# A GRU between two expert layers: chunk 0's early sums in f16 parts, idle f16 passes, and new places for y, routing and evacuation

## The chip, the cores and the metric

The kernel runs on one core of a Trainium2 chip. The metric is the device time of one execution in microseconds (us); the runs of a kernel are summed up by their median. The core's engines work side by side, each in the order of its own instruction stream, and wait for one another by semaphores: PE (TensorE, matmuls), ACT (ScalarE), DVE (VectorE), POOL (GpSimd) and SP (which issues DMAs).

## What is computed

Sixteen sequences of 128 time steps with 128 features, in two layers with a residual each:

```python
h  = gelu(x @ W.T + fc_bias + (x @ v / 128) @ u.T / 16 + cond)     # low-rank adapted, exact gelu
x  = x + relu(h @ q(W1).T + b1) @ q(W2).T + b2                      # q: weights rounded to -1, 0, 1
def step(H, xt):                                                    # a GRU over the 128 time steps
    Z  = sigmoid(xt @ Wxz.T + bxz + H @ Whz.T + bhz)
    R  = sigmoid(xt @ Wxr.T + bxr + H @ Whr.T + bhr)
    Ht = tanh(xt @ Wxh.T + bxh + R * H @ Whh.T + bhh)
    H  = Z * H + (1 - Z) * Ht
    return H, H @ Whq.T + bhq
y  = scan(step, cond, x)
e  = argmax(y @ router_w.T + router_b)                              # one of 32 experts for each token
x  = x + relu(relu(y @ w1[e] + b1[e]) @ w2[e] + b2[e])
```

## The kernel before, in words

Features lie on the 128 partitions, and a column is one (time, sequence) pair, so a time step is 16 columns. The 128 steps are cut into K = 8 chunks of 16 steps, 256 columns each. The GRU is one chain of 128 steps; all other work is hung into the chain's gaps. While chunk k runs its steps, the first layer (gelu and ternary FFN) is worked out for chunks k+1 to k+3, and routing and experts for chunk k-1. The order on every engine is written out by hand: each step of each engine calls functions that look at k and t (the step in the chunk) and issue what stands there.

A step goes like this. PE adds x's share to the sum for the early copy of the reset gate (`early_input`, L948), then the old state's products with the gates' weights (`product`, L1082, and `early_product`, L959). ACT takes three sigmoids (L454 r_early, L458 the gate r into `factors`, L460 z), DVE forms r * H in f16 (`terms`, L837) and, by a scan, the rounding error of that (`parts`, L866). PE multiplies both with Whh into the candidate's sum; ACT makes keep = 1 - z (L482) and tanh (L487); DVE forms the two halves z * H and keep * tanh of the new state, each as an f16 value and an f16 remainder (`zh_p` L871 and L876, `m_p` L880 and L883), and PE goes on with those.

The other work has three places in a step on PE: `before` (behind the gates' products, ahead of `terms`), `between` (`terms` and `parts`), and `behind` (behind `parts`, while tanh and the state's update run); in chunk 0 these are `first_before`, `first_between` and `first_behind`. On DVE the places are behind `terms` and ahead of the scan, `wide(k, t, 0)` in the middle (ahead of `zh_p`'s remainder, L876) and `wide(k, t, 1)` at the step's end; chunk 0 has `first_early` and `first_wide`. On ACT they are behind z, ahead of keep and tanh, and behind tanh.

Numbers of full precision go through PE as two f16 parts (value and remainder, `_hi` and `_lo`), with three products. In chunk 0 those parts of x do not exist, and its products with x, in `early_input` and `project_first` (L963), are f32 matmuls on x itself. `spare_passes`, `spare_hidden` and `stream` (L1130) are matmuls of 256 f16 columns into halves of PSUM banks that nobody reads; they compute nothing that is used. `x1_evacuate` (L525) takes the ternary FFN's sum out of the O bank and adds the residual; `early_input` writes to the same bank, and where the bank is being read (`out_bank_read`, L1126) PE first waits for `zh_lo`, which DVE signals behind the evacuation. `y_high` (L364) makes y's f16 value from the Whq product, `y_low` its remainder; `best_logit`, `best_places` and `first_place` find the best expert; `turn_masks` (PE) and `turned_masks` (ACT) make the mask. `expert_low` makes the remainder of an expert tile, half a tile at a time, and PE's `expert_hidden` for tile c waits for both halves of tile c - 2 (L1006).

## Time and profile before

| | |
|---|---|
| median of 3 runs | 259.83 us (259.51 to 261.93) |
| the profiled execution | 263.02 us, of which the span is 261.2 us |
| PE busy in the span | 250.5 us (96%), 3854 matmuls |
| DVE, ACT busy | 218.3 us (84%), 162.7 us (62%) |
| granted clock of PE, mean over the span | 0.928 |

All engines' times are counted from the span's start. A busy time of PE is modelled from when matmuls start, and matmuls overlap, so the distance from one matmul's start to the next one's tells more of what it costs than its own duration. The granted clock is the share of full speed (2.4 GHz) that PE was given. The step borders in the tables below are the starts of r's sigmoid (L458).

### The profile page before, as it was taken

Reading aid. Unit: us, or ns where it says so; the run is one execution under the profiler, and the core shown is the slowest. Engines: PE = TensorE matmul, PEld = TensorE weight load, DVE = VectorE, ACT = ScalarE, POOL = GpSimd, SP = SyncE. Lnnn points to the kernel's source line nnn. Section 1 sums busy time; section 2 is a strip of 40 time slices with the busy share of each in tenths; the row PEclk is TensorE's granted clock in tenths of the full one; section 3 lists DMA queues with packets and bytes.
Section 4 is the critical chain, followed back from the end, with each engine's and each line's share of the span. In section 5 each row is a group of like instructions: output and inputs, shape, how many; then the busy total and the mean of one; then the engine's idle time right before and its main releaser. Section 6 shows DMA issues by size and latency. Waiting matters only on the chain.

```text
span 261.2 us, 10662 instructions
## 1 busy us (share of the span) xinstructions
PE 250.5 (96%) x3854; PEld 204.6 (78%) x3854; DVE 218.3 (84%) x1528; ACT 162.7 (62%) x826; POOL 15.2 (6%) x29
## 2 busy tenths in 40 slices
PE   6999899999999999999999999999999999999996
PEld 6978788788877788788877777777877777777775
DVE  5776566789998989988998999898988988788983
ACT  3455455557665866677666766587657766556652
POOL 4872000000000000000000000000000000000000
PEclk9995555559999999999999999999999999999999
DMA  7900000000000000000000000000000000000000
GB/s 245 360 15 6 0 3 1 3 0 4 4 3 4 23 1 3 4 24 3 4 4 20 4 3 4 4 23 4 3 1 23 4 4 3 21 5 0 5 23 23
DMA packets 3380, 5.76 MB, mean 22 GB/s; under 512 B 568, under 2 KB 2128, under 8 KB 3328
## 3 DMA queue, kind: packets, MB, share of 16 engines
q1 hardware_dynamic: 2848, 4.24, 4.8%
q10 hardware_dynamic: 432, 0.74, 0.8%
q8 instruction: 31, 0.51, 0.8%
q14 instruction: 21, 0.17, 0.2%
q0 software_dynamic: 48, 0.10, 0.1%
HBM read 4.03 MB, written 1.05 MB: 19 GB/s over the span
## 4 chain that ended last, share of the span: by engine, by line
PE 83%; DVE 10%; ACT 3%; issue 2%; DMA 2%; DVEq 0%
PE ZH L1087 9%; PE R L1087 8%; PE F L1010 6%; PE O L960 6%; PE ZH L1086 5%; PE O L957 3%; DVE parts L866 3%; PE O L916 3%; PE L L1097 2%; PE R L1132 2%; PE L L982 2%; PE O L953 2%; PE O L917 2%; PE O L918 2%; PE R L1086 2%
## 5 line engine op out<-in xcount | busy, mean ns | idle before, releaser
L454 ACT ACTIVATE r_early<-O 128x16 f32<-128x16 f32 x127 | 23.5, 185 | 35.0 <-PE O L960 32.0
L1087 PE MATMUL R<-m_p,gru_hi 128*128 128x16 f16 x254 | 44.2, 175 | 0.0
L487 ACT ACTIVATE ZH<-ZH 128x16 f32<-128x16 f32 x128 | 21.8, 170 | 29.9 <-PE ZH L1087 28.1
L1087 PE MATMUL ZH<-m_p,gru_hi 128*128 128x16 f16 x254 | 36.7, 170 | 0.0
L866 DVE TENSOR_TENSOR_SCAN parts<-factors,terms 128x48 f16<-128x48 f32 x128 | 33.0, 258 | 4.1 <-ACT factors L458 0.5
L837 DVE TENSOR_TENSOR terms<-r_early,factors 128x16 f16<-128x16 f32 x128 | 24.0, 188 | 12.7 <-ACT r_early L454 8.0
L609 DVE SCALAR_TENSOR_TENSOR hid_lo<-F,hid_hi 128x128 f16<-128x128 f32 x112 | 31.9, 285 | 0.2 <-issue 0.2
L458 ACT ACTIVATE factors<-R 128x16 f32<-128x16 f32 x128 | 24.7, 193 | 11.5 <-PE R L1087 0.2
L880 DVE TENSOR_TENSOR m_p<-keep,ZH 128x16 f16<-128x16 f32 x128 | 21.8, 170 | 11.4 <-ACT ZH L487 7.1
L482 ACT ACTIVATE keep<-z_sb 128x16 f32<-128x16 f32 x128 | 28.3, 221 | 2.1
L1086 PEld LDWEIGHTS ZH<-terms,gru_lo 128*128 128x128 f16 x128 | 12.7, 100 | 18.4 <-ACT z_sb L460 15.5
L1087 PE MATMUL R<-zh_p,gru_hi 128*128 128x16 f16 x254 | 26.0, 170 | 0.2 <-DVE zh_p L876 0.2
L883 DVE TENSOR_TENSOR m_p<-m,m_p 128x16 f16<-128x16 f32 x128 | 22.5, 176 | 4.3
L1087 PEld LDWEIGHTS R<-m_p,gru_hi 128*128 128x128 f16 x254 | 24.5, 96 | 2.0
L1087 PE MATMUL ZH<-parts,gru_hi 128*128 128x16 f16 x128 | 23.7, 185 | 1.7 <-DVE parts L866 0.7
L1087 PE MATMUL ZH<-zh_p,gru_hi 128*128 128x16 f16 x254 | 24.8, 170 | 0.0
L1086 PE MATMUL ZH<-terms,gru_lo 128*128 128x16 f16 x128 | 23.6, 184 | 1.0 <-ACT z_sb L460 0.3
L1087 PEld LDWEIGHTS ZH<-m_p,gru_hi 128*128 128x128 f16 x254 | 23.7, 98 | 0.0
L951 PE MATMUL O<-ones,gbias 128*128 128x16 f16 x127 | 22.6, 178 | 0.8 <-DVE zh_p L876 0.5
L960 PE MATMUL O<-m_p,gru_hi 128*128 128x16 f16 x127 | 22.9, 181 | 0.4
L460 ACT ACTIVATE z_sb<-ZH 128x16 f32<-128x16 f32 x128 | 23.0, 180 | 0.2 <-PE ZH L965 0.2
L885 DVE TENSOR_TENSOR factors<-zh,m 128x16 f32<-128x16 f32 x128 | 22.4, 175 | 0.0
(270 smaller groups left out, 1057.3 us busy)
## 6 DMA issues: line engine op xcount, KB each, us to landing
w_sb<-w SPq DMA_DIRECT2D x2, 512.0 KB, 8.1
outT<-res SPq DMA_DIRECT2D x7, 128.0 KB, 1.9
xs_sb<-xsT SPq DMA_DIRECT2D x1, 640.0 KB, 9.7
first_sb<-first ACTq DMA_DIRECT2D x1, 279.0 KB, 4.0
ffn_sb<-ffn SPq DMA_DIRECT2D x1, 256.0 KB, 3.8
ffn_sb<-ffn ACTq DMA_DIRECT2D x1, 256.0 KB, 4.8
second_sb<-second SPq DMA_DIRECT2D x1, 256.0 KB, 4.5
xs_sb<-xsT SPq DMA_DIRECT2D x1, 256.0 KB, 6.7
```

The source lines that it names most:

```text
L454: nc.scalar.activation(r_early[:, p, :], early_r[:, at], ACT.Sigmoid).then_inc(early_made, 1)
L458: nc.scalar.activation(factors[:, step % (2 * STEPS), :, 2], r_in, ACT.Sigmoid).then_inc(r_made, 1)
L460: nc.scalar.activation(z_sb[:, p, :], z_in, ACT.Sigmoid).then_inc(z_made, 1)
L482: nc.scalar.activation(keep[:, p, :], z_sb[:, p, :], ACT.Copy, bias=1.0, scale=-1.0).then_inc(keep_made, 1)
L609: nc.vector.scalar_tensor_tensor(out=hid_lo[:, c % 4, at], in0=F_bank[c % 2][:, at], scalar=0.0, in1=hid_hi[:, c % 4, at], op0=ALU.max, op ...
L837: nc.vector.tensor_tensor(terms[:, p, :, 2], r_early[:, p, :], h_old, ALU.mult).then_inc(rh_hi, 1)
L866: nc.vector.tensor_tensor_scan(parts[:, p].rearrange("p b s -> p (b s)"), factors[:, now].rearrange("p b s -> p (b s)"), terms[:, p].rearr ...
L883: nc.vector.tensor_tensor(m_p[:, q, 1, :], m[:, q, :], m_p[:, q, 0, :], ALU.subtract).then_inc(m_lo, 1)
L951: mm(out, gbias[:, 0:C], ones16[:, 0:B], start=False, stop=False, skip_group_check=True)
L960: return mm(early_r[:, t * B:(t + 1) * B], gru_hi[:, WHR, :], part, start=False, stop=False, skip_group_check=True)
L1086: mm(out, gru_lo[:, WHR + gate, :], part, start=False, stop=False, skip_group_check=True)
L1087: return mm(out, gru_hi[:, WHR + gate, :], part, start=False, stop=low, skip_group_check=True)
```

## The change

`early_input` in chunk 0 takes x as f16 parts from step 4 on; x's parts for that are made in two halves (`x1_first_high` on ACT, `x1_first_low` on DVE). In chunk 0, 25 idle f16 passes of 256 columns are added: `spare_first` ahead of and between the candidate's products, and more `spare_passes` behind them. To make room, casts and remainders of the experts' weights (w1_high, w2_high, w2_low) and `twice_gelu(2)` change places in chunk 0. In the later chunks `y_high` moves from ahead of keep and tanh to behind tanh, `x1_high` from step 7 to 8; on DVE y_low, ffn_low, best_places and the first-place operations get other places, `x1_evacuate` is cut into two halves of 128 columns (one in the middle of step 6, one early in step 7), and from there `expert_low(0)`, `x1_low` and `low_rank_masked` stand one place later.

```diff
                 def x1_high(n):
-                act.wait_ge(x1_made, n + 1)
+                act.wait_ge(x1_made, 2 * n + 1)
...
+            def x1_first_high(half):
+                if half == 1:
+                    act.wait_ge(x1_rest_made, 1)
+                at = slice(half * 128, half * 128 + 128)
+                nc.scalar.copy(x1_hi[:, 0, at], x1[:, at]).then_inc(x1_first_hi, 1)
...
-                    if experts and t == 0:
-                        y_high(k - 1)
...
+                    if k == 0 and t == 6:
+                        x1_first_high(1)
...
-                    if feed and t == (13 if k == 0 else 7):
+                    if feed and t == (13 if k == 0 else 8):
                         x1_high(k + 1)
...
+                    if k == 0 and t == 2:
+                        x1_first_high(0)
...
+                    if experts and t == 0:
+                        y_high(k - 1)
...
+            def x1_first_low(half):
+                dve.wait_ge(x1_first_hi, half + 1)
+                at = of(half)
+                nc.vector.tensor_tensor(x1_lo[:, 0, at], x1[:, at], x1_hi[:, 0, at],
+                                        ALU.subtract).then_inc(x1_first_lo, 1)
...
+                if t == 7:
+                    x1_first_low(1)
...
+                if t == 2 and half == 1:
+                    x1_first_low(0)
...
-                if t == 1:
-                    y_low(k - 1, half)
-                if 2 <= t < 2 + NF:
+                if t == 1 and half == 0:
+                    y_low(k - 1, 0)
+                if t == 1 and half == 1:
+                    ffn_low(k + 1, 0, 0)
+                if t == 2:
+                    ffn_low(k + 1, half, 1 - half)
+                if t == 3 and half == 0:
+                    best_places(k - 1, 0)
+                if t == 3 and half == 1:
+                    ffn_low(k + 1, 1, 1)
+                if t in (4, 5):
                     ffn_low(k + 1, t - 2, half)
-                if t == 3:
-                    best_places(k - 1, half)
-                if t == 4 and half == 0:
-                    first_place(k - 1, 1)
...
-                    x1_evacuate(k + 1)
-                if 7 <= t < 15 and half == 0:
+                    x1_evacuate(k + 1, 0)
...
+                if t == 7:
+                    expert_low(k - 1, 0, half)
+                if 8 <= t < 15 and half == 0:
                     expert_low(k - 1, t - 7, 1)
...
+                        if t == 2:
+                            y_low(k - 1, 1)
                         if t == 4:
-                            first_place(k - 1, 0)
-                        if 7 <= t < 15:
+                            best_places(k - 1, 1)
+                        if t == 5:
+                            first_places(k - 1)
+                        if t == 7:
+                            x1_evacuate(k + 1, 1)
+                        if 8 <= t < 15:
                             expert_low(k - 1, t - 7, 0)
...
-                if k == 0:
+                if k == 0 and t < 4:
                     mm(out, gru_sb[:, WXR, :], x1[:, at], start=False, stop=False, skip_group_check=True)
                 else:
+                    if k == 0 and t in (4, 8):
+                        pe.wait_ge(gru_lo_made, 2)
+                        pe.wait_ge(x1_first_lo, 1 + t // 8)
                     hi, lo = x1_hi[:, k % 2, at], x1_lo[:, k % 2, at]
...
+            def spare_first(passes):
+
+                stream(L_bank[:, N:2 * N], passes)
+
             def first_before(t, step):
+                if t > 1:
+                    spare_first({2: 1, 3: 1, 6: 2, 7: 1, 12: 2, 13: 4}.get(t, 0))
...
             def first_between(t):
+                if t in (4, 10, 11, 12, 13):
+                    spare_first(1)
...
-                spare_passes(0, {7: 1, 8: 0, 9: 1, 12: 3, 13: 3}.get(t, 0))
+                spare_passes(0, (1, 1, 1, 1, 1, 1, 0, 1, 1, 1, 1, 1, 3, 3, 0, 0)[t])
```

On PE, chunk 0's step 4, from the work ahead of the candidate's products to the next step's early sum, stood before as follows (xs_sb and second_sb are f32, `R<-low` is the low-rank product of chunk 1's gelu):

```order
L1102 MATMUL R<-xs_sb,second_sb 128x64
L1113 MATMUL R<-low,second_sb 128x16x8
L1086 MATMUL ZH<-terms,gru_lo 128x16
L1087 MATMUL ZH<-terms,gru_hi 128x16
L1087 MATMUL ZH<-parts,gru_hi 128x16
L1113 MATMUL R<-low,second_sb 128x16x8
L951 MATMUL O<-ones,gbias 128x16
L953 MATMUL O<-x,gru_sb 128x16
```

and stands now:

```order
L1147 MATMUL R<-xs_sb,second_sb 128x64
L1158 MATMUL R<-low,second_sb 128x16x8
L1131 MATMUL ZH<-terms,gru_lo 128x16
L1132 MATMUL ZH<-terms,gru_hi 128x16
L1177 MATMUL L<-gru_hi 128x256
L1132 MATMUL ZH<-parts,gru_hi 128x16
L1158 MATMUL R<-low,second_sb 128x16x8
L1177 MATMUL R<-gru_hi 128x256
L993 MATMUL O<-ones,gbias 128x16
L1002 MATMUL O<-x_hi,gru_lo 128x16
L1002 MATMUL O<-x_hi,gru_hi 128x16
L1002 MATMUL O<-x_lo,gru_hi 128x16
```

Two idle passes (L1177) came in, and three f16 products take the place of the f32 one.

On ACT, the first step of a later chunk, from z to the next step's first sigmoid, before:

```order
L460 ACTIVATE z_sb<-ZH 128x16
L366 ACTIVATE y_hi<-L,first_sb 128x256
L482 ACTIVATE keep<-z_sb 128x16
L487 ACTIVATE ZH<-ZH 128x16
L454 ACTIVATE r_early<-O 128x16
```

and now:

```order
L467 ACTIVATE z_sb<-ZH 128x16
L491 ACTIVATE keep<-z_sb 128x16
L496 ACTIVATE ZH<-ZH 128x16
L367 ACTIVATE y_hi<-L,first_sb 128x256
L461 ACTIVATE r_early<-O 128x16
```

The y evacuation moved behind keep and tanh (ZH<-ZH).

On DVE, step 7 of a later chunk, from terms to the step's last operation, before (hid_lo is `expert_low(0)`, one row for each half):

```order
L837 TENSOR_TENSOR terms<-r_early,factors 128x16
L609 SCALAR_TENSOR_TENSOR hid_lo<-F,hid_hi 128x128
L866 SCALAR_TENSOR_TENSOR parts<-factors,terms 128x48
L871 TENSOR_TENSOR zh_p<-z_sb,factors 128x16
L872 TENSOR_TENSOR zh<-z_sb,factors 128x16
L609 SCALAR_TENSOR_TENSOR hid_lo<-F,hid_hi 128x128
L876 TENSOR_TENSOR zh_p<-zh,zh_p 128x16
L880 TENSOR_TENSOR m_p<-keep,ZH 128x16
L881 TENSOR_TENSOR m<-keep,ZH 128x16
L883 TENSOR_TENSOR m_p<-m,m_p 128x16
L885 TENSOR_TENSOR factors<-zh,m 128x16
L553 TENSOR_TENSOR x_lo<-x,x_hi 128x128
```

and now:

```order
L875 TENSOR_TENSOR terms<-r_early,factors 128x16
L542 SCALAR_TENSOR_TENSOR x<-O,first_sb,xs_sb 128x128
L908 SCALAR_TENSOR_TENSOR parts<-factors,terms 128x48
L913 TENSOR_TENSOR zh_p<-z_sb,factors 128x16
L914 TENSOR_TENSOR zh<-z_sb,factors 128x16
L631 SCALAR_TENSOR_TENSOR hid_lo<-F,hid_hi 128x128
L918 TENSOR_TENSOR zh_p<-zh,zh_p 128x16
L922 TENSOR_TENSOR m_p<-keep,ZH 128x16
L923 TENSOR_TENSOR m<-keep,ZH 128x16
L925 TENSOR_TENSOR m_p<-m,m_p 128x16
L927 TENSOR_TENSOR factors<-zh,m 128x16
L631 SCALAR_TENSOR_TENSOR hid_lo<-F,hid_hi 128x128
```

The evacuation's second half stands where the first hid_lo stood, and the two hid_lo moved to the middle and the end of the step.

## Rows read from the trace of the kernel before

**Rows 1.** The page, part 2: granted clock in tenths, 40 slices of 6.5 us.

```profile
PEclk9995555559999999999999999999999999999999
```

**Rows 2.** Busy time by chunk (stretch, length, engines' busy us and instructions, granted clock): chunks 0, 3.

```profile
14.52:53.79 39.27, 37.62 (x419) 32.59 (x419) 27.14 (x182) 21.48 (x110) 6.00 (x14) 0.57 0.01 2
...
111.39:139.49 28.10, 27.82 (x468) 22.36 (x468) 25.61 (x190) 19.48 (x101) 0.00 (x0) 1.00 0.03 8
```

**Rows 3.** The same view of chunk 0: steps 0 and 1, 2, 3, 4, 5, 12 to 15.

```profile
14.52:18.57 4.05, 3.97 (x55) 3.39 (x55) 3.39 (x21) 2.93 (x16) 3.21 (x9) 1.00 0.01 4
18.57:20.37 1.80, 1.80 (x27) 1.56 (x27) 1.52 (x11) 1.34 (x8) 1.55 (x4) 0.88 0.02 6
20.37:23.16 2.79, 2.79 (x27) 2.66 (x28) 1.69 (x10) 1.32 (x8) 1.25 (x3) 0.50 0.01 2
23.16:25.72 2.56, 2.55 (x26) 2.33 (x26) 1.57 (x11) 1.22 (x7) 0.00 (x0) 0.50 0.04 10
25.72:29.66 3.94, 2.84 (x28) 2.67 (x29) 1.84 (x12) 1.33 (x7) 0.00 (x0) 0.50 0.00 0
45.04:53.79 8.75, 8.30 (x101) 6.38 (x102) 6.85 (x47) 4.84 (x26) 0.00 (x0) 0.50 0.01 2
```

**Rows 4.** The same view: chunk 1's steps 0 and 1; chunk 4's steps 0, 1, 4, 6.

```profile
53.79:58.17 4.38, 4.38 (x59) 3.77 (x60) 3.39 (x23) 2.58 (x13) 0.00 (x0) 0.58 0.00 0
...
139.49:141.50 2.01, 1.97 (x31) 1.70 (x32) 1.48 (x12) 1.10 (x6) 0.00 (x0) 1.00 0.00 0
141.50:143.20 1.70, 1.70 (x30) 1.36 (x30) 1.67 (x13) 1.46 (x7) 0.00 (x0) 1.00 0.23 77
...
146.93:148.80 1.87, 1.80 (x29) 1.40 (x28) 1.84 (x17) 1.47 (x7) 0.00 (x0) 1.00 0.00 0
...
150.56:152.38 1.82, 1.75 (x32) 1.37 (x31) 1.46 (x11) 1.22 (x7) 0.00 (x0) 1.00 0.03 9
```

**Rows 5.** Timeline of PE (start, duration, engine, line): f32 early sums and what follows.

```profile
17.68 0.37 PE L953 MATMUL O<-x,gru_sb 128*128 128x16 f32 x2
17.90 0.17 PE L960 MATMUL O<-zh_p,gru_hi 128*128 128x16 f16 x1
...
28.71 0.59 PE L953 MATMUL O<-x,gru_sb 128*128 128x16 f32 x2
29.14 0.17 PE L960 MATMUL O<-zh_p,gru_hi 128*128 128x16 f16 x1
```

**Rows 6.** Timeline of PE: idle passes (L1132), f16 early sums, at either clock.

```profile
142.30 0.27 PE L1132 MATMUL R<-gru_hi 128*128 128x256 f16 x1
142.41 0.17 PE L951 MATMUL O<-ones,gbias 128*128 128x16 f16 x1
...
142.51 0.17 PE L960 MATMUL O<-zh_p,gru_hi 128*128 128x16 f16 x1
...
48.08 0.80 PE L1132 MATMUL R<-gru_hi 128*128 128x256 f16 x3
48.67 0.22 PE L951 MATMUL O<-ones,gbias 128*128 128x16 f16 x1
```

**Rows 7.** Timeline, chunk 0's step 5: the gelu product, and PE's wait.

```profile
26.35 0.41 DVE L547 SCALAR_TENSOR_TENSOR g<-erf,R 128x256 f32<-128x256 f32 x1
...
26.82 0.39 PE L945 MATMUL R<-ones,gbias 128*128 128x256 f16 x1 [1.11 <-DVE g L547]
```

**Rows 8.** Timeline, chunk 4's step 0: ACT's y evacuation and tanh, PE's candidate product.

```profile
140.08 0.47 ACT L366 ACTIVATE y_hi<-L,first_sb 128x256 f16<-128x256 f32 x1 [0.33 <-PE L L982]
...
140.56 0.17 ACT L487 ACTIVATE ZH<-ZH 128x16 f32<-128x16 f32 x1
...
140.15 0.17 PE L1087 MATMUL ZH<-parts,gru_hi 128*128 128x16 f16 x1
```

**Rows 9.** Timeline, chunk 4: the end of step 7 on DVE, step 8's expert product.

```profile
153.91 0.28 DVE L553 TENSOR_TENSOR x_lo<-x,x_hi 128x128 f16<-128x128 f32 x1
...
154.02 0.27 PE L1010 MATMUL F<-y_hi,w_lo 128*128 128x256 f16 x1
```

More of the change, by code:

```diff
@@ L492, in _ @@
                         first_relu(1, 2 * t + 1)
-                    if k == 0 and t in (2, 3, 6):
-                        w1_high((2, 3, 6).index(t))
+                    if k == 0 and t == 2:
+                        x1_first_high(0)
+                    if k == 0 and t in (3, 6):
+                        w1_high((3, 6).index(t) * 2)
+                    if k == 0 and t == 15:
+                        w2_high(3)
                     if k == 0 and t == 4:
@@ L523, in of, with x1_evacuate @@
                 return slice(half * 128, half * 128 + 128)
-            def x1_evacuate(n):
+            def x1_evacuate(n, half):
                 dve.wait_ge(ffn_out_mm, n)
-                nc.vector.scalar_tensor_tensor(out=x1[:, cols(n)], in0=O_bank[:, 0:N], scalar=vec[:, V_B2:V_B2 + 1],
-                                               in1=xs(n), op0=ALU.add, op1=ALU.add).then_inc(x1_made, 1)
+                nc.vector.scalar_tensor_tensor(out=x1[:, cols(n)][:, of(half)], in0=O_bank[:, of(half)],
+                                               scalar=vec[:, V_B2:V_B2 + 1], in1=xs(n)[:, of(half)], op0=ALU.add,
+                                               op1=ALU.add).then_inc(x1_made, 1)
             def x1_first(half):
@@ L597, in above, with first_places @@
                                                       in1=total, op0=ALU.mult, op1=ALU.is_ge)
-            def first_place(q, i):
-                if i == 0:
-                    dve.wait_ge(key_made, 2 * q + 2)
-                if q == 0 and i == 0:
+            def first_places(q):
+                dve.wait_ge(key_made, 2 * q + 2)
+                if q == 0:
                     dve.wait_ge(zeros_set, 2)
-                above(blocks(pen[:, i, :]), key[:, i:i + 1, :], best[:, i:i + 1]).then_inc(pen_made, 1)
+                for i in range(2):
+                    above(blocks(pen[:, i, :]), key[:, i:i + 1, :], best[:, i:i + 1]).then_inc(pen_made, 1)
             def expert_low(q, c, half):
@@ L756, in first_wide @@
                     ffn_low(1, t - 8, half)
+                if t == 2 and half == 1:
+                    x1_first_low(0)
                 if t == 12 and half == 0:
                     dve.wait_ge(xs_next_in, 16)
-                    x1_evacuate(1)
+                    x1_evacuate(1, 0)
+                if t == 12 and half == 1:
+                    twice_gelu(2, 1)
                 if t == 14:
@@ L780, in wide @@
                         dve.wait_ge(xs_in, 16)
-                    x1_evacuate(k + 1)
-                if 7 <= t < 15 and half == 0:
+                    x1_evacuate(k + 1, 0)
+                if k == 1 and t == 6 and half == 1:
+                    w2_low(7)
+                if t == 7:
+                    expert_low(k - 1, 0, half)
+                if 8 <= t < 15 and half == 0:
                     expert_low(k - 1, t - 7, 1)
-                if t in (7, 8) and half == 1:
-                    x1_low(k + 1, t - 7)
-                if t in (9, 10) and half == 1 and k < K - 3:
-                    low_rank_masked(k + 3, t - 9)
+                if t in (8, 9) and half == 1:
+                    x1_low(k + 1, t - 8)
+                if t in (10, 11) and half == 1 and k < K - 3:
+                    low_rank_masked(k + 3, t - 10)
                 if t in (12, 13) and half == 1 and k < K - 2:
@@ L801, in wide_last @@
                     best_places(K - 2, 1)
-                if t == 3 and half == 1:
-                    first_place(K - 2, 0)
                 if t - 1 in LAST_HIDDEN_AT and half == 0:
@@ L847, in _ @@
                         finish(k - 2, 1)
-                    if k == 0 and t in (12, 13):
-                        twice_gelu(2, t - 12)
                     if k == 0 and t in (14, 15):
@@ L853, in _ @@
                         first_early(t)
-                    if k == 1 and t in (0, 2, 6):
-                        w2_low((0, 2, 6).index(t) + 5)
+                    if k == 1 and t in (0, 1, 6):
+                        w2_low((0, 1, 6).index(t) + 4)
                     if last:
@@ L859, in _ @@
                         if t == 4:
[L860 removed]
+                            first_places(k - 1)
                         if t - 1 in LAST_HIDDEN_AT:
@@ L1021, in expert_bias2 @@
                 if q < K - 2:
-                    pe.wait_ge(x1_made, q + 3)
+                    pe.wait_ge(x1_made, 2 * q + 5)
                 for i in range(3):
```

16 lines of the change are left out of this document (11 added, 5 removed).

## The prediction

> **What bounds the kernel now.** I read the page's clock line first: TensorE (PE) holds full clock nearly everywhere, but six of the 40 slices show half [rows 1]. The busy table cut by chunks places them: chunk 0 takes 39.27 us at a mean granted clock of 0.57, chunk 3 28.10 us at 1.00 [rows 2]. Both run the same 16 recurrent steps, so chunk 0 is 11 us longer than its sister. Cut by steps, it falls apart [rows 3]: steps 0 and 1 take 4.05 us together at full clock, step 2 1.80 (the fall to 1.2 GHz, the lower of the two levels, comes at its end), step 3 2.79 us at half clock and busy all the time, step 5 3.94 us. Chunk 1's first two steps still take 4.38 us; the clock comes back in the second [rows 4]. Elsewhere a step costs 1.70 us when nothing is in its way: the recurrent chain of PE, ACT (ScalarE) and DVE (VectorE). Chunk 4's steps 0, 4 and 6 take 2.01, 1.87 and 1.82 [rows 4]. So there are two stocks: chunk 0's clock, and a few tenths in some steps of every later chunk.
>
> What PE did before the fall: from step 0 on it was busy 3.97 of 4.05 and 1.80 of 1.80 us, in steps 1 and 2 with the recurrent 16-column products, four f32 products a step and no f16 pass of 256 columns (counted in the code). Before the rise it ran chunk 1's first steps, with six and five such passes. Chunks 2 to 6 have three to eight in every step, and kept the clock. The change gives chunk 0's steps 1 to 5 one or two, its steps 6 to 15 three to eight.
>
> **The change, part by part.**
>
> *Early sums.* An f32 early sum holds PE from 17.68 to 17.90, 0.22 us at full clock, and from 28.71 to 29.14, 0.43 us, at half [rows 5]. A bias and three f16 products hold it from 142.41 to 142.51 [rows 6]; three of four is some 0.07 at full clock, 0.10 at half. So steps 4 to 15 win 0.15 us of PE time each at full clock and 0.33 at half. The parts cost two casts on ACT and two subtractions on DVE of 128 columns, in slots emptied for them or, in step 2, at the end, where DVE waits for the next gate anyway. PE's new waits in steps 4 and 8 are for work two steps and one step old, so I put them at nothing; without that cover a subtraction, 0.28 us [rows 9], once each.
>
> *Idle passes.* There are 25 in chunk 0. One holds PE 0.11 us at full clock (142.30 to 142.41) and 0.20 at half (three from 48.08 to 48.67) [rows 6]. At full clock a step has room: the later chunks fit eight passes into 1.70 us. The exception are steps 0 to 3, still with f32 sums, where PE itself is last: I add 0.08, 0.08, 0.10 and 0.10. All 25 on the path would be 2.7 us, none of them nothing.
>
> *What the clock gives back, if it stays.* Steps 0 to 3: 4.05 + 0.16, and twice 1.80 + 0.10, together 8.01 against 8.64. In step 5 PE waits 1.11 us for the gelu product on DVE, which sits behind that step's scan [rows 7]; ACT and DVE don't slow with PE's clock, and the change leaves this wait in place. The other 2.83 us halve where they are PE's, to some 1.6: 2.7 against 3.94. Steps 4 and 6 to 15 are 39.27 - 8.64 - 3.94 = 26.69 us; at 1.80 each, between the 1.70 and 1.87 of chunk 4, 19.8. Chunk 0 becomes 30.5: **-8.8 us** (at 1.70 a step -9.9, at 1.95 -7.2). Chunk 1's first two steps become 2.0 and 1.7: **-0.7**.
>
> *y behind the tanh.* At a chunk's start ACT runs the y evacuation, 0.47 us, ahead of keep and tanh, which starts at 140.56. Its product was issued at 140.15 and takes 0.17 [rows 8]; with 0.06 until a waiter starts (PE starts at 26.82 what DVE ended at 26.76 [rows 7]) tanh could start at 140.38. So -0.18 in each of chunks 1 to 7: **-1.3**. What is late next: the y evacuation ends 0.3 us later, but its first reader on DVE stands a step later.
>
> *Routing and evacuation in new places* (chunks 1 to 6). Step 4 loses one DVE operation ahead of terms (it now follows terms, where DVE waits for r), step 3 one ahead of m_p. Step 6's evacuation is halved, and PE's wait for the bank with it. Excess over 1.70: 0.17 and 0.12 in steps 4 and 6 [rows 4], some 0.05 in step 3; I take all of it, -0.34 a chunk. Steps 2 and 5 get an operation more ahead of the scan, +0.09 together. **A new wait**: the first expert tile's second half moves from the middle of step 7 to its end, to the place of the operation at 153.91. PE's expert product of step 8, issued at 154.02 [rows 9], needs it: 153.91 + 0.28 + 0.06 = 154.25. Behind it in PE's queue stand that tile's four passes, the candidate product and the rest of the step; so +0.22 in chunks 1 to 4, where a low-rank product follows, and little in 5 and 6, whose slot is empty. Sum: 6 x (-0.34 + 0.09) + 4 x 0.22 = **-0.6**; none of the gains and all the waits would be +1.4, the gains alone -2.0. Chunk 7 gets both place operations in one slot and empties another: nothing.
>
> *The sum*: -8.8 - 0.7 - 1.3 - 0.6 = -11.4. The profiled execution took 263.02 us, 261.2 of it span and 1.8 around it; it becomes 251.6. The median of the three runs shown is 259.83, 3.2 lower. I forecast on the median's scale: 259.83 - 11.4 = **248.4 us**.
>
> **A rule against it.** The rows first: PE was busy 3.97 of 4.05 and 1.80 of 1.80 us when the clock fell [rows 3]; the one long idle time, 1.11 us, comes later [rows 7]. The Trainium skill's page "TensorE: Matmul & The Clock Gate", section "HAM oscillation — how this bites in real kernels", names idle gaps between matmuls as what throttles the clock. By that rule passes into a busy engine change nothing, and the sum is rival two's. The trace disagrees, since the fall came without such a gap. That more passes keep the clock, no run shows yet.
>
> **Rivals.**
> 1. *The clock stays until step 5 and falls there.* The 1.11 us wait remains, and no pass stands in it. For: it is the longest hole in the chunk, and steps 4 and 5 carry just two wide passes each. Against: step 6 follows with seven. Steps 0 to 4 win 1.4 us (0.63, and 2.56 to 1.80), step 5 some 0.7. At half clock steps 6 to 15 win ten times 0.33 by the f16 sums and pay 16 passes of 0.20: even. With the 1.9 of the later chunks, -4.0: 255.8. If the dense steps 12 and 13 bring the clock back, steps 12 to 15 (8.75 us [rows 3] against 7.0) and chunk 1's 0.7 come on top, -6.4: 253.4.
> 2. *The passes don't hold it; it falls in step 2 as before.* Twelve f16 sums save 12 x 0.33 = 4.0, 25 passes cost 5.0, the later chunks give 1.9: -0.9, or **258.9**. For: until then only steps 0 to 2 have changed, by one, one and two passes.
> 3. *Slower.* The fall of rival two, with all 25 half-clock passes on PE's path (5.0), while the f16 sums save nothing because m_p is last in their place: 5.0 - 1.9 = +3.1, 262.9. It is slower by over 1% from 23 passes of 0.20 us on. Against: half-clock steps such as 3 show PE without idle time [rows 3], so a shorter sum must count too.
>
> **How the numbers follow.** 1%, 2.6 us, is about what a measurement of this kernel can tell from no change. The forecast, with its bounds 246.5 to 251 (chunk 0's -9.9 with the gains alone; its -7.2 with half the later gains), gets 0.50: the steps that lost the clock are lifted towards those that kept it. Rival one gets 0.33 (251 to 256.5), since its hole is real and the rows can't rule it out. Rival two gets 0.11 (within 1%), rival three 0.06. So faster 0.83, same 0.11, slower 0.06. The range reaches over the first two: 246.5 to 256.5.
>
> **What would show it.** Right: the clock line is full over chunk 0, its 16 steps take 30 to 31 us, step 5 about 2.7 with its wait for DVE; tanh at a chunk's start follows its product by 0.23; PE waits some 0.2 us for the second hid_lo in step 8 of chunks 1 to 4. Wrong: half clock from step 5 on (rival one), or from step 2 (rivals two and three), when chunk 0 takes 35 us and more; or chunk 3 above its 28.1 us, if the new waits outweigh the new places.

## The result, and the profile after

The changed kernel takes 251.48 us (median of 4 runs, 251.42 to 251.56), the kernel before 260.88 us beside it (4 runs, 259.51 to 261.98): a ratio of 0.964, interval 0.958 to 0.970. The profiled execution took 251.42 us, 249.6 of it span; the span before was 261.2 us.

The page of the changed kernel, its first line and the granted clock in tenths over 40 slices (here of 6.24 us), answers to [rows 1]:

```profile
span 249.6 us, 10749 instructions
...
PEclk9999799999999999999999999999999999999999
```

The six half-clock slices are gone; one slice, the fifth, shows a dip. Busy time by stretch (stretch, length, engines' busy us and instructions, granted clock), chunk 0, then its steps 0 and 1, 2, 3, 4, 5, 6 and 7, answers to [rows 2, 3]:

```profile
14.32:45.30 30.98, 29.64 (x456) 25.09 (x456) 26.80 (x185) 21.72 (x112) 6.20 (x14) 0.94 0.01 3
...
14.32:18.21 3.89, 3.82 (x57) 3.35 (x56) 3.13 (x20) 2.94 (x15) 2.88 (x8) 1.00 0.02 4
18.21:20.25 2.04, 2.04 (x29) 1.82 (x28) 1.84 (x11) 1.22 (x7) 1.79 (x4) 1.00 0.02 4
20.25:22.29 2.04, 2.04 (x31) 1.81 (x30) 1.86 (x12) 1.33 (x7) 1.53 (x4) 1.00 0.02 3
22.29:23.99 1.70, 1.69 (x29) 1.39 (x29) 1.50 (x12) 1.40 (x7) 0.00 (x0) 1.00 0.07 14
23.99:26.88 2.89, 1.81 (x30) 1.71 (x31) 1.83 (x13) 1.33 (x7) 0.00 (x0) 0.95 0.00 0
26.88:29.44 2.56, 2.56 (x31) 2.17 (x30) 1.65 (x13) 1.22 (x7) 0.00 (x0) 0.50 0.00 0
29.44:31.39 1.95, 1.95 (x30) 1.84 (x30) 1.70 (x13) 1.46 (x8) 0.00 (x0) 0.85 0.00 0
```

Chunk 0 went from 39.27 to 30.98 us. Its first five steps hold full clock. The clock falls at the end of step 5, behind the hole (the time in which PE stands idle and waits for the gelu product), and is back within step 7. The hole is nearly as long as before ([rows 7]: 1.11 us; timeline of PE, after):

```profile
25.07 0.28 PE L987 MATMUL R<-ones,gbias 128*128 128x256 f16 x1 [1.09 <-DVE g L569]
```

The steps of chunks 0, 1 and 4, from one r sigmoid to the next, in us, worked out from the starts of that line on ACT (L458 before, L465 after), to about 0.01:

```
                t=0    1    2    3    4    5    6    7    8    9   10   11   12   13   14   15
chunk 0 before 1.92 2.12 1.80 2.80 2.56 3.94 2.55 2.67 2.45 2.59 2.56 2.56 2.38 2.28 2.18 1.91
        after  2.01 1.88 2.04 2.04 1.70 2.89 2.56 1.95 1.78 1.70 1.70 1.70 1.77 1.86 1.70 1.70
chunk 1 before 2.45 1.93 1.78 1.75 1.88 1.76 1.87 1.81 1.81 1.70 1.70 1.70 1.70 1.70 1.99 1.70
        after  1.72 1.71 1.80 1.70 1.70 1.78 1.74 1.84 1.99 1.70 1.70 1.70 1.70 1.70 1.70 1.70
chunk 4 before 2.01 1.70 1.75 1.98 1.87 1.76 1.82 1.80 1.81 1.70 1.70 1.70 1.77 1.70 1.70 1.70
        after  1.80 1.71 1.80 1.70 1.70 1.76 1.70 1.82 1.99 1.70 1.70 1.70 1.70 1.70 1.70 1.70
```

Three rows of chunk 4's step 0 (timeline, start and duration) answer to [rows 8]: the candidate's last product, tanh, and the y evacuation, now behind it.

```profile
130.00 0.17 PE L1132 MATMUL ZH<-parts,gru_hi 128*128 128x16 f16 x1
...
130.20 0.17 ACT L496 ACTIVATE ZH<-ZH 128x16 f32<-128x16 f32 x1 [0.36 <-PE ZH L1132]
...
130.28 0.47 ACT L367 ACTIVATE y_hi<-L,first_sb 128x256 f16<-128x256 f32 x1
```

Tanh starts 0.20 us behind the start of its product, where it had been 0.41. And the new wait in step 8 of the same chunk (timeline, PE's weight load for the expert product; it answers to [rows 9]):

```profile
143.07 0.28 DVE L631 SCALAR_TENSOR_TENSOR hid_lo<-F,hid_hi 128x128 f16<-128x128 f32 x1
...
143.41 0.10 PEld L1055 LDWEIGHTS F<-y_hi,w_lo 128*128 128x128 f16 x1 [0.17 <-DVE hid_lo L631]
```

### The profile page after: what moved, and what is told of

It reads as the page before. It is cut to its first block, busy times and chain, and to the rows that moved or that the text cites. A ratio compares the mean times of both kernels' runs of the same rounds, so it can differ in the third digit from the quotient of the medians.

```text
span 249.6 us, 10749 instructions
## 1 busy us (share of the span) xinstructions
PE 240.7 (96%) x3891; PEld 196.7 (79%) x3891; DVE 218.1 (87%) x1537; ACT 162.9 (65%) x828; POOL 15.3 (6%) x29
## 4 chain that ended last, share of the span: by engine, by line
PE 88%; DVE 6%; ACT 2%; issue 2%; DMA 2%; DVEq 0%
PE ZH L1132 10%; PE R L1132 8%; PE F L1055 7%; PE O L1005 6%; PE ZH L1131 6%; PE O L1002 3%; PE F L1177 3%; PE R L1177 3%; PE O L958 3%; PE L L1142 2%; PE L L1027 2%; PE O L959 2%; PE O L960 2%; PE R L1131 2%; PE F L1061 2%; PE R L1158 2%
## 5 line engine op out<-in xcount | busy, mean ns | idle before, releaser
L1132 PE MATMUL R<-m_p,gru_hi 128*128 128x16 f16 x254 | 44.4, 176 | 0.0
L1132 PE MATMUL ZH<-m_p,gru_hi 128*128 128x16 f16 x254 | 37.5, 169 | 0.0
L465 ACT ACTIVATE factors<-R 128x16 f32<-128x16 f32 x128 | 24.7, 193 | 12.4
L1132 PEld LDWEIGHTS R<-m_p,gru_hi 128*128 128x128 f16 x254 | 24.3, 96 | 2.1
L1132 PE MATMUL R<-zh_p,gru_hi 128*128 128x16 f16 x254 | 24.8, 169 | 0.0
L1132 PE MATMUL ZH<-zh_p,gru_hi 128*128 128x16 f16 x254 | 24.7, 169 | 0.0
L1132 PEld LDWEIGHTS ZH<-m_p,gru_hi 128*128 128x128 f16 x254 | 24.1, 97 | 0.0
L1131 PE MATMUL ZH<-terms,gru_lo 128*128 128x16 f16 x128 | 23.1, 181 | 0.9 <-DVE terms L875 0.2
L1132 PE MATMUL ZH<-parts,gru_hi 128*128 128x16 f16 x128 | 23.4, 182 | 0.7
L914 DVE TENSOR_TENSOR zh<-z_sb,factors 128x16 f32<-128x16 f32 x128 | 22.3, 175 | 0.1
L993 PE MATMUL O<-ones,gbias 128*128 128x16 f16 x127 | 22.0, 173 | 0.3
## 6 DMA issues: line engine op xcount, KB each, us to landing
ffn_sb<-ffn SPq DMA_DIRECT2D x1, 256.0 KB, 3.6
ffn_sb<-ffn ACTq DMA_DIRECT2D x1, 256.0 KB, 4.7
second_sb<-second SPq DMA_DIRECT2D x1, 256.0 KB, 4.4
xs_sb<-xsT SPq DMA_DIRECT2D x1, 256.0 KB, 6.6
```

What stands on the lines that cost most here:

```text
L465: nc.scalar.activation(factors[:, step % (2 * STEPS), :, 2], r_in, ACT.Sigmoid).then_inc(r_made, 1)
L914: nc.vector.tensor_tensor(zh[:, q, :], z_sb[:, p, :], h_old, ALU.mult).then_inc(zh_full, 1)
L1131: mm(out, gru_lo[:, WHR + gate, :], part, start=False, stop=False, skip_group_check=True)
L1132: return mm(out, gru_hi[:, WHR + gate, :], part, start=False, stop=low, skip_group_check=True)
```

## The experiments

The question is what holds the clock in chunk 0 (the passes, the shorter sums, or both), what the hole in step 5 costs, and what each later move is worth by itself. In all kernels the idle passes compute nothing that is used, so that none of the edits leaves out a part of the computation. The kernel before has medians of 260.88 us beside the changed kernel, 262.0 beside e1 to e4, 262.27 beside e5 to e8 and 262.3 beside e9 to e12; times of different groups are therefore compared by their steps first.

**e1_no_passes**: the changed kernel without the 25 passes.

```diff
-                    spare_first({2: 1, 3: 1, 6: 2, 7: 1, 12: 2, 13: 4}.get(t, 0))
+                    spare_first(0)
...
-                if t in (4, 10, 11, 12, 13):
-                    spare_first(1)
...
-                spare_passes(0, (1, 1, 1, 1, 1, 1, 0, 1, 1, 1, 1, 1, 3, 3, 0, 0)[t])
+                spare_passes(0, {7: 1, 8: 0, 9: 1, 12: 3, 13: 3}.get(t, 0))
```

> The changed kernel without its 25 idle passes; chunk 0's early sums stay in f16 parts from step 4 on, and all places stay as changed. Theory (the passes hold the clock): PE falls to half clock in step 2 or 3, as in the kernel before, and stays there until chunk 1's first steps; the twelve f16 sums save 0.33 us each at half clock, so chunk 0 takes about 39.3 - 4.0 = 35.3 us instead of 31.0, chunk 1's first two steps lose 0.7 to 1.0 again: 251.5 + 4.3 + 0.8 = 256.6 us (255 to 258). Rival (the shorter sums are what did it, the passes are idle in every sense): full clock over chunk 0, steps 0 to 3 some 0.1 to 0.2 us shorter each, 250.5 to 251.5 us.

256.0 us (255.57 to 256.69, 4 runs), ratio to before 0.978 (0.973 to 0.983). The page's clock line:

```profile
PEclk9995555579999999999999999999999999999999
```

Busy time of chunk 0, its step 2, and steps 3 to 14, in which the twelve sums stand (each step issues the next one's), then the same steps in the kernel before:

```profile
14.16:49.40 35.24, 33.42 (x431) 28.86 (x431) 27.21 (x184) 21.52 (x112) 6.12 (x14) 0.58 0.01 3
17.91:19.80 1.89, 1.89 (x26) 1.67 (x26) 1.71 (x11) 1.22 (x7) 1.64 (x4) 0.94 0.02 4
...
19.80:47.36 27.56, 25.85 (x324) 22.26 (x324) 20.82 (x143) 16.26 (x85) 1.62 (x4) 0.50 0.01 3
```

```profile
20.37:51.88 31.51, 29.94 (x313) 26.24 (x314) 20.51 (x140) 16.38 (x83) 1.25 (x3) 0.50 0.01 2
```

As the theory had it: without the passes the clock falls at the end of step 2, as in the kernel before, while PE is busy 1.89 of 1.89 us. Steps 3 to 14 are at half clock from end to end in both kernels and take 27.56 us instead of 31.51: 0.33 us for each of the twelve f16 sums, as forecast. (The moved casts are in this figure too; no run parts them.)

**e2_passes_only**: the kernel before with the 25 passes and nothing else.

```diff
...
+                if t > 1:
+                    spare_first({2: 1, 3: 1, 6: 2, 7: 1, 12: 2, 13: 4}.get(t, 0))
...
+                if t in (4, 10, 11, 12, 13):
+                    spare_first(1)
...
-                spare_passes(0, {7: 1, 8: 0, 9: 1, 12: 3, 13: 3}.get(t, 0))
+                spare_passes(0, (1, 1, 1, 1, 1, 1, 0, 1, 1, 1, 1, 1, 3, 3, 0, 0)[t])
```

> The kernel before with the 25 idle passes alone (f32 early sums in all of chunk 0, all other places as before). Theory (the passes hold the clock): full clock over chunk 0 but for at most a few us behind step 5's stall; the f32 sums cost twelve times 0.15 us, the later chunks lack their 1.9 us: 251.5 + 1.8 + 1.9 = 255.2 us (254 to 257). Rival (the shorter sums are needed for the clock): half clock from step 2 or 3 on, with the passes on PE's path at 0.20 us: no faster than before, 260 to 265 us.

260.88 us (257.84 to 261.62, 10 runs), ratio 0.995 (0.991 to 0.999). The theory's 254 to 257 us failed; the time lies in the rival's range (260 to 265), but not for the rival's reason, since the clock did not fall in step 2 or 3. The clock line:

```profile
PEclk9999555699999999999999999999999999999999
```

Busy time of chunk 0 and its step 5:

```profile
14.19:53.11 38.92, 37.53 (x444) 32.37 (x444) 26.84 (x183) 21.42 (x111) 6.19 (x14) 0.69 0.01 2
24.20:27.59 3.39, 2.29 (x29) 2.09 (x30) 1.84 (x13) 1.32 (x8) 0.00 (x0) 0.80 0.00 0
```

The passes do carry the clock through steps 0 to 4, so that part of the theory holds. It falls in step 5, as in the changed kernel, but with f32 sums it stays down through step 13 (steps 6 to 13 take 2.59 to 2.99 us, step 14 1.77), and there the passes themselves are on the path: steps 10 and 11 take 2.99 where the kernel before has 2.56. So the passes alone win next to nothing: steps 2 to 5 save 1.7 us, and steps 6 to 13 pay 2.0.

**e3_fill_stall**: the changed kernel with 8 more passes in the hole.

```diff
-                    spare_first({2: 1, 3: 1, 6: 2, 7: 1, 12: 2, 13: 4}.get(t, 0))
+                    spare_first({2: 1, 3: 1, 5: 8, 6: 2, 7: 1, 12: 2, 13: 4}.get(t, 0))
```

> The changed kernel with 8 more idle passes at the head of step 5 in chunk 0, where PE waits 1.09 us for the gelu product; 8 of 0.11 us fit into that. Theory (this hole is what made the clock fall for 3.4 us in step 6): full clock over the whole of chunk 0; step 6 2.56 to about 1.75, step 7 1.95 to 1.80, step 5 2.89 to 2.8: 251.5 - 1.0 = 250.5 us (250.2 to 250.8). Rival one (something else makes it fall there): the clock line as before this edit, 251.5 us. Rival two (the passes delay the work behind them): step 5 longer by 0.1 us and more, 251.5 to 252.

249.96 us (249.76 to 250.28, 4 runs), ratio 0.955 (0.951 to 0.959); the theory had 250.2 to 250.8. Timeline of PE in step 5:

```profile
23.57 1.03 PE L1177 MATMUL L<-gru_hi 128*128 128x256 f16 x8
...
24.81 0.28 PE L987 MATMUL R<-ones,gbias 128*128 128x256 f16 x1 [0.20 <-DVE g L569]
```

Busy time of chunk 0 and its step 6:

```profile
13.69:44.04 30.35, 29.73 (x464) 24.73 (x464) 26.68 (x185) 21.71 (x112) 6.14 (x14) 1.00 0.02 4
24.74:26.51 1.77, 1.70 (x30) 1.65 (x31) 0.70 (x7) 0.66 (x3) 0.00 (x0) 1.00 0.00 0
```

Full clock from end to end (by run, 0.999 to 1.00); step 6 takes 1.77 us instead of 2.56 and step 7 1.78 instead of 1.95, together 0.96, and step 5 itself is no longer (2.88). With eight passes in the hole the clock no longer falls. This run both closes the hole and adds wide matmuls, and eight more passes elsewhere were not tried; that the hole itself counts, e5_gelu_first shows below, where it is halved without a pass.

**e4_y_front** and **e7_y_front_filled**: the y evacuation ahead of keep and tanh again, in the changed kernel and in e3_fill_stall.

```diff
+                    if experts and t == 0:
+                        y_high(k - 1)
                     if k == 0 and t < 2:
...
-                    if experts and t == 0:
-                        y_high(k - 1)
                     if experts and t == (4 if last else 5):
```

> The changed kernel with the y evacuation back ahead of keep and tanh in the first step of chunks 1 to 7. Theory (it held tanh up): each of these steps becomes 0.18 us longer, 1.80 to 1.98: 251.5 + 1.3 = 252.8 us (252.4 to 253.1). Rival (the first steps became shorter by something else, the clock in chunk 1 or the work moved on DVE): 251.3 to 251.7 us.

> e3_fill_stall with the y evacuation ahead of keep and tanh again, so that chunk 0's clock, which spread e4_y_front's runs, stays out of it. Theory (the evacuation held tanh up): the first steps of chunks 1 to 7 from 1.78 to 1.96 us, 249.96 + 1.3 = 251.25 us (251.0 to 251.5). Rival (only chunk 0 and 1's clock made e4_y_front slower): 249.8 to 250.2 us.

e4_y_front: 252.93 us (252.06 to 254.88, 4 runs). The total agrees with the theory, but not for its reason alone: the edit touches nothing in chunk 0, and yet the profiled execution has 34.19 us there, since the clock that fell in step 5 came back only in step 10. Busy time of chunk 0, step 5, steps 6 to 9:

```profile
13.46:47.65 34.19, 32.64 (x456) 27.54 (x456) 27.26 (x185) 21.72 (x112) 6.06 (x14) 0.80 0.02 6
23.33:27.12 3.79, 2.71 (x30) 2.48 (x31) 1.83 (x12) 1.33 (x7) 0.00 (x0) 0.62 0.00 0
27.12:36.64 9.52, 9.52 (x116) 8.36 (x115) 6.88 (x49) 5.65 (x29) 0.00 (x0) 0.50 0.01 2
```

Here the clock fell while the hole was still open (busy time of 0.5 us of it, clock 0.74; PE starts again at 24.41), and not 1.5 us behind its end as in the changed kernel:

```profile
24.00:24.50 0.50, 0.09 (x1) 0.09 (x2) 0.44 (x3) 0.00 (x1) 0.00 (x0) 0.74 0.00 0
```

The mean clock of its four runs is 0.973, 0.986, 0.993 and 0.993, so with the same chunk 0 the fall costs now more, now less; why, no run shows. With the hole filled, e7_y_front_filled takes 251.65 us (251.48 to 252.26, 4 runs; forecast 251.0 to 251.5) at a clock of 1.00 in each. Its chunk 4, step 0 (busy time), stands against 1.80 us in the changed kernel:

```profile
129.46:131.47 2.01, 1.97 (x31) 1.70 (x32) 1.49 (x12) 1.09 (x6) 0.00 (x0) 1.00 0.03 8
```

Over chunks 1 to 7 the two profiled executions differ by 0.23, 0.21, 0.08, 0.22, 0.23, 0.24 and 0.09, together 1.30 us: what was forecast for y. (Chunk 3 gains less, since its step 1 is 0.08 us longer with y behind the tanh, and chunk 7, since its step 0 gains 0.09 only.)

**e5_gelu_first**: the changed kernel with the hole halved. On DVE the gelu product of step 5 goes ahead of the scan, and a remainder of the experts' weights takes its place.

```diff
-                if t in (4, 5, 10, 11):
-                    w2_low((4, 5, 10, 11).index(t))
+                if t == 5:
+                    twice_gelu(1)
+                if t in (4, 10, 11):
+                    w2_low({4: 0, 10: 2, 11: 3}[t])
...
                 if t == 5 and half == 0:
-                    twice_gelu(1)
+                    w2_low(1)
```

> The changed kernel (without the filling passes of e3_fill_stall) with chunk 0's step 5 turned around on DVE: the gelu product goes ahead of the scan, in the place of a remainder of the experts' weights, which goes where the gelu product was. PE's wait shrinks from 1.09 to about 0.5 us and step 5 from 2.89 to about 2.4. Theory (the length of that hole decides whether the clock falls): no fall in step 6, another 1.0 us: 250.0 us (249.7 to 250.4), in every run alike. Rival one (any hole there is enough): half clock behind step 5 as before, 251.0 us, and runs apart by up to 3 us. Rival two (the scan, now later by 0.1 to 0.2 us, is what PE waits for): step 5 not shorter, 251.5 us.

249.55 us (249.52 to 252.47, 4 runs; forecast 249.7 to 250.4), ratio 0.955 (0.948 to 0.961). PE's wait in step 5 (timeline):

```profile
24.14 0.28 PE L989 MATMUL R<-ones,gbias 128*128 128x256 f16 x1 [0.55 <-DVE g L569]
```

And the step (busy time):

```profile
23.60:25.94 2.34, 1.80 (x31) 1.74 (x32) 1.80 (x13) 1.32 (x8) 0.00 (x0) 1.00 0.00 0
```

Step 5 falls from 2.89 to 2.34, and the clock stays in three runs of four (1.00). In the fourth, 252.47 us, the mean clock was 0.98: the theory's "in every run alike" is wrong. With a hole of 0.55 us one run of four lost the clock for a time, with 1.09 us all four of the changed kernel. That the rest of the hole is what cost that one run is not shown: there is no profile of it.

**e6_evac_back**: e3_fill_stall with the evacuation in one piece in step 6 and the work that had moved behind it one place earlier.

```diff
...
-                    x1_evacuate(k + 1, 0)
+                    x1_evacuate_all(k + 1)
...
-                        if t == 7:
-                            x1_evacuate(k + 1, 1)
-                        if 8 <= t < 15:
+                        if 7 <= t < 15:
                             expert_low(k - 1, t - 7, 0)
...
-                if t == 7:
-                    expert_low(k - 1, 0, half)
-                if 8 <= t < 15 and half == 0:
+                if 7 <= t < 15 and half == 0:
                     expert_low(k - 1, t - 7, 1)
```

> e3_fill_stall with the evacuation of the ternary sum in one piece of 256 columns in step 6 again (chunks 1 to 6), and expert_low, x1_low, low_rank_masked and x1_high one place earlier, as in the kernel before. Theory (the new place made the wait in step 8): step 8 of chunks 1 to 4 from 1.99 to 1.81 us, step 6 of chunks 3 to 6 from 1.70 to 1.82 and of chunks 1 and 2 from 1.75 to 1.87: 6 x 0.12 - 4 x 0.18 = 0.0, 249.9 us against e3_fill_stall's 249.96; the change's split won nothing. Rival (step 8 waits for something else): step 8 stays at 1.99 and the time rises by 0.7, 250.7 us.

250.11 us (249.79 to 250.69, 4 runs) against 249.96. Busy time of chunk 4's steps 6 and 8 here, then the same two in e3_fill_stall:

```profile
138.98:140.88 1.90, 1.75 (x32) 1.36 (x31) 1.54 (x11) 1.21 (x6) 0.00 (x0) 1.00 0.00 0
142.68:144.48 1.80, 1.80 (x32) 1.51 (x31) 1.63 (x14) 1.12 (x6) 0.00 (x0) 1.00 0.03 9
```

```profile
138.51:140.21 1.70, 1.70 (x32) 1.39 (x31) 1.37 (x12) 1.21 (x7) 0.00 (x0) 1.00 0.00 0
142.03:144.02 1.99, 1.93 (x32) 1.76 (x33) 1.63 (x14) 1.31 (x8) 0.00 (x0) 1.00 0.00 0
```

The split wins 0.20 us in step 6 and loses 0.19 in step 8. In chunks 5 and 6 it wins in step 6 and has no loss in step 8. Chunks 1 to 6 differ by 0.2 us in all (167.5 against 167.3), less than the runs can tell.

**e8_f32_filled**: e3_fill_stall with f32 early sums in all of chunk 0.

```diff
-                if k == 0 and t < 4:
+                if k == 0:
                     mm(out, gru_sb[:, WXR, :], x1[:, at], start=False, stop=False, skip_group_check=True)
```

> e3_fill_stall with f32 early sums in all of chunk 0 (the parts of x are still made). Theory (with the hole filled the passes alone hold the clock, and an f32 sum costs 0.15 us of PE time that is on the path): full clock over chunk 0, its steps 4 to 15 longer by 0.15 each: 249.96 + 1.8 = 251.8 us (251.0 to 252.2). Rival one (the shorter sums are needed for the clock too): half clock in parts of chunk 0, 254 us and more. Rival two (PE has room for them at full clock): 250.0 us.

251.26 us (251.03 to 251.81, 4 runs). Busy time of steps 4 to 15, in this kernel and in e3_fill_stall:

```profile
22.09:44.90 22.81, 22.45 (x340) 18.62 (x341) 20.37 (x144) 16.24 (x84) 0.00 (x0) 1.00 0.01 3
```

```profile
22.04:44.04 22.00, 21.60 (x351) 17.77 (x351) 19.82 (x144) 16.22 (x83) 0.00 (x0) 1.00 0.01 3
```

Full clock with f32 sums too, so with the hole filled the passes alone hold it. The eleven sums that stand in these steps cost 0.81 us, 0.07 each and not 0.15: about half of their PE time is not on the path at full clock.

**e11_before_filled**: the kernel before with the 25 passes and 8 in the hole (e2_passes_only with `5: 8` in the table, as in e3_fill_stall).

> The kernel before with the 25 idle passes and 8 more in step 5's wait, nothing else: all places as before, f32 early sums in all of chunk 0. Theory (the length of the half clock in e2_passes_only came from step 5's hole alone): full clock over chunk 0, which takes about 30.9 us as in e8_f32_filled; the later chunks lack the 1.3 us of y and some 0.6 of the other places: 251.3 + 1.9 = 253.2 us (252.7 to 253.8). Rival (without the f16 sums and the moves the passes do not carry the clock): half clock in parts of chunk 0 again, 256 to 262 us.

253.57 us (253.42 to 253.8, 4 runs), ratio 0.969 (0.964 to 0.974), against 260.88 without the eight; the mean clock is 1.00 in three runs and 0.993 in one. Busy time of chunk 0:

```profile
14.13:45.24 31.11, 30.46 (x452) 25.72 (x452) 26.61 (x183) 21.45 (x111) 6.12 (x14) 1.00 0.01 3
```

Theory confirmed: 33 matmuls that compute nothing bring chunk 0 from 39.27 to 31.11 us, and the eight in the hole decide.

**e9_gelu_fill**: e5_gelu_first with 4 passes in what is left of the hole (`5: 4` in the table). **e10_fewer_early**: the same without the passes ahead of `terms` in steps 2 and 3.

```diff
-                    spare_first({2: 1, 3: 1, 5: 4, 6: 2, 7: 1, 12: 2, 13: 4}.get(t, 0))
+                    spare_first({5: 4, 6: 2, 7: 1, 12: 2, 13: 4}.get(t, 0))
```

> e5_gelu_first with 4 idle passes in what is left of PE's wait in chunk 0's step 5 (some 0.5 us; 4 of 0.11 us fit). Theory (a hole of any length there is a risk to the clock, and the turned order is worth its 0.5 us by itself): full clock in every run, step 5 at 2.34, 249.5 us (249.2 to 249.8) with no run above 250. Rival one (the passes now delay the candidate's products): step 5 2.45 and more, 249.7 to 250. Rival two (the one run of e5_gelu_first at 252.47 us had another cause than the hole): a run above 251.5 us again.

> e9_gelu_fill without the two idle passes ahead of terms in chunk 0's steps 2 and 3, which stood at 1.89 to 2.27 us in the runs so far; one pass behind the candidate's products remains in each. Theory (PE is last in these steps, and what is left keeps the clock): steps 2 and 3 shorter by 0.1 to 0.2 us together, full clock: 249.3 us (249.0 to 249.6). Rival one (these two passes are needed): half clock from step 3 or 4 on in some or all runs, 251 to 256 us. Rival two (the steps wait for DVE, which POOL's work slows, not for PE): no change, 249.5 us.

e9_gelu_fill: 249.85 us (249.64 to 250.43, 4 runs), ratio 0.955 (0.948 to 0.962); every run has a mean clock of 0.999 or 1.00, and chunk 0 (busy time) is the second shortest of all, with e10_fewer_early's profiled 29.31:

```profile
14.45:43.93 29.48, 29.07 (x460) 24.46 (x460) 26.48 (x185) 21.72 (x113) 6.16 (x14) 1.00 0.01 3
```

Step 5 is 2.34 us as without the four passes, so they cost nothing. The theory's 249.2 to 249.8 with no run above 250 was missed: two runs lie above it (250.03 and 250.43). By their medians this kernel, e3_fill_stall and e5_gelu_first cannot be told apart, and the 0.5 us that it gains on e3_fill_stall is shown by step 5 alone. The run that e5_gelu_first had at 252.47 us did not come again, but no loss in four runs beside one in four proves little. e10_fewer_early: 251.4 us (249.8 to 252.71, 4 runs), with mean clocks of 1.00, 0.979, 0.979 and 1.00. Two of four runs lost the clock for a time: rival one, "in some or all runs". Nor did steps 2 and 3 become shorter in the profiled execution: 1.91 and 1.93 us in both kernels. But step 2 goes from 1.86 to 2.23 us in the profiled executions of kernels with the same chunk 0 up to there, so that a cost of 0.1 us can't be excluded. Four runs against four don't show that the two passes are needed. For it speaks that in the seven kernels that keep them and have the hole filled, 27 of 28 runs have a mean clock of at least 0.999 (one of e11_before_filled has 0.993).

**e12_routing_back**: e3_fill_stall with DVE's routing work in chunks 1 to 6 where it was before.

```diff
...
+                if t == 3:
+                    best_places(k - 1, half)
+                if t == 4 and half == 0:
+                    first_place(k - 1, 1)
...
-                        if t == 2:
-                            y_low(k - 1, 1)
                         if t == 4:
-                            best_places(k - 1, 1)
-                        if t == 5:
-                            first_places(k - 1)
+                            first_place(k - 1, 0)
```

> e3_fill_stall with DVE's routing work (y_low, best_places, the first-place operations, and the remainders that changed places with them) of chunks 1 to 6 where the kernel before had it; the evacuation stays in halves. Theory (the places win what the step table shows): step 4 from 1.70 to 1.87, step 3 from 1.70 to 1.75, step 2 from 1.80 to 1.75, so 0.17 a chunk: 249.96 + 1.0 = 251.0 us (250.7 to 251.3). Rival (step 4's gain comes from something else): 249.8 to 250.2 us.

250.7 us (250.6 to 252.33, 4 runs, all at a clock of 1.00) against 249.96. Busy time of chunk 4's step 4, 1.70 us in the changed kernel:

```profile
137.20:139.07 1.87, 1.80 (x29) 1.40 (x28) 1.83 (x17) 1.46 (x7) 0.00 (x0) 1.00 0.03 9
```

Steps 2, 3 and 4 go to 1.74, 1.75 and 1.87 in each chunk, 0.16 longer together, as the theory had it. In chunk 5 a single step gains 0.35 (2.06 to 1.71, see the last section), so the sum over chunks 1 to 6 is 0.6 us.

## Why the prediction was right, and where it was not

The time lies in the range, the direction was right, and the sum was nearly exact trace against trace: -11.4 forecast, 261.2 to 249.6, that is -11.6, measured. In part that is luck: chunk 0 gave 8.3 us of the 8.8, chunks 1 to 7 gave 3.0 instead of 2.6, and 0.3 lies ahead of the first step and behind the last one, where nothing was forecast. The single time of 248.4 was 3.1 us too low. And 251.48 lies outside the forecast's own bounds (246.5 to 251) and inside rival one's (251 to 256.5); the range held because it reached over both. (The lower bound is mis-added: -9.9 - 0.7 - 1.3 - 2.0 gives 245.9. Nothing hangs on it.) Point by point:

**What bounds it.** Right: chunk 0 was 11 us longer than its sister, most of it for its clock, and giving the clock back took it from 39.27 to 30.98. e11_before_filled shows it without the rest of the change: at full clock the old chunk 0 takes 31.11 us, so that 8.2 of the 11 us were the clock, and 3 were not.

**The clock if it stays.** Steps 0 to 3 were put at 8.01 us and took 7.97; step 5 at 2.7 and took 2.89; steps 4 and 6 to 15 at 19.8 and took 20.12. But *that* it stays is what the forecast claimed, and it did not: it fell where rival one said, behind the 1.11 us hole of [rows 7]. What rival one had wrong is how long: it put the clock back at step 12 at the earliest, and it was back in step 7. In the changed kernel's four runs alike the mean clock is 0.993, and by e3_fill_stall the fall costs 0.96 us. e4_y_front shows that the short fall was luck in part, with the clock down until step 10 and 34.19 us for the same chunk 0. The step that failed is the choice of the clock's two pure cases; the forecast's 1.80 us a step was wide enough to swallow a short one.

**The early sums.** At half clock right (0.33 us each in e1_no_passes, as forecast). At full clock 0.07, not the 0.15 of PE time. What the prediction didn't see is what stands behind the hole: with f32 sums, the old places and the same passes the clock comes back in step 14 (e2_passes_only), with f16 sums and the new places in step 7, or in step 10 (e4_y_front). Which of the two does it, the sums or the places, no run parts. Passes alone -1.1 us against before, sums alone -6.0 (both by medians beside the 262.0 of the same chip; the sums' figure has the later chunks' moves in it), both together -9.4 (beside 260.88): more than their sum with the hole open, though by hardly more than the noise of the three ratios.

**Idle passes.** Right that they hide at full clock where there is room: steps 4, 10 and 11 got two each and take 1.70 us. For steps 2 and 3, where 0.10 each was added, the runs can't tell. Right, too, that at half clock they are on the path (e2_passes_only).

**y behind the tanh.** Right in place and size: -0.18 in step 0 on average, from -0.10 to -0.22 (11.84 to 10.74 us over chunks 2 to 7), 1.30 us in all. Not seen: 0.08 given back in chunk 3's step 1. Chunk 7's step 1 is longer too (1.71 to 1.77), but not by y: it is as long in e7_y_front_filled, and 1.70 in e6_evac_back.

**Routing and evacuation.** Each forecast step shows: step 4 to 1.70, step 3 to 1.70, step 2 up by 0.05, step 6 to 1.70 to 1.77, and step 8 is longer by 0.18 to 0.20 for the new wait in chunks 1 to 4 (forecast 0.22), and not in 5 and 6. The routing's places won 0.16 us in each chunk, about 1.0 in all, of which the slow step of chunk 5 took 0.35 back (e12_routing_back); the split evacuation won nothing (e6_evac_back). That this comes to the -0.6 of the sum is luck in part. Chunk 7 was put at y's -0.18 and became 0.23 us longer (26.42 to 26.65 up to its last r sigmoid): one step, told of below, is 0.33 longer, the others are 0.10 shorter together.

**The scale.** This is the step that put the single time off. The profiled execution stood 3.2 us above the median of the runs shown, and I took the whole gain from that median. But what set the runs of before apart went, with one exception, with the length of the half-clock stretch that the change removes: in the 27 runs of the kernel before beside the experiments, those at a mean clock of 0.922 to 0.928 have spans of 260.2 to 261.4 us, those at 0.934 and 0.947 spans of 258.0 to 259.1, but for one of 261.1 at 0.934. A run with a shorter half-clock stretch had less to win. On the profiled execution's own scale the same sum gives 263.02 - 11.4 = 251.6, and 251.48 was measured.

**The rule on idle gaps.** The Trainium skill's page "TensorE: Matmul & The Clock Gate", section "HAM oscillation — how this bites in real kernels", names idle gaps as what throttles the clock. Both sides of the weighing came true in part. The fall in step 2 needs no gap: in e1_no_passes PE is busy 1.89 of 1.89 us, and passes put into that busy engine prevented it, against the sum that I worked out by the page's rule. The fall in step 5 is nearer to the page's case: the gap of 1.09 us was followed by it, and with the gap filled it was gone. But the waits in the page's example are several times as long as this gap, so that the trace goes further here than the rule.

## What to carry to other kernels

Cut the granted clock by stage before anything else: a stage that does the same work as its sisters at half clock was the largest stock here (8.2 us of 261), and a few wide matmuls that compute nothing, put where PE is busy with narrow ones and above all into its holes, may give it back. Fill the hole as well as the busy stretch, and look at every run's mean clock, since a kernel near the edge loses it in some runs only. When the gain lies in a stretch that itself varies from run to run, take the sum against the execution from which the durations were read, and not against the median.

Several versions beat both kernels, and the medians of the best three (249.55, 249.85 and 249.96 us) can't be told apart. The one to take is e9_gelu_fill: the gelu product ahead of the scan in step 5, with four passes in what is left of the wait, 249.85 us and a mean clock of at least 0.999 in each of its four runs.
